# Last weighting of the first cross-attention in four pieces by queries, with spare products moved and added

## The reference

```
q = (layernorm(x) @ wq)  -> 16 heads of 64
k = (ctx @ wk)           -> 16 heads of 64
v = (ctx @ wv)           -> 16 heads of 16
attn = softmax(q k^T / 8)             # 128 queries x 12544 keys, per head
x = x + concat_heads(attn @ v)        # 128 x 256
x = x + attention(layernorm(x)) ...   # next stage, needs all of x
```

## Time and profile before

| | us |
|---|---|
| median of 3 runs | 947.75 |
| lowest, highest run | 946.58, 948.14 |
| profiled execution, its own time | 947.57 |
| its span in the trace | 945.8 |
| what lies around the span (difference) | 1.8 |
| PE busy in the span | 923.0 (98%) |
| first cross-attention in the trace | 0 to about 629 |

### The profile page before, as it was taken

One profiled execution on the slowest core, in us unless ns is written; L12 is line 12 of the kernel. 1 busy time (PEld: TensorE's weight loads), 2 busy tenths in 40 slices (PEclk: granted clock), 3 DMA queues, 4 the chain that ended last, 5 costly groups with the idle time before them and its releaser, 6 DMA issues.

```text
span 945.8 us, 30864 instructions
## 1 busy us (share of the span) xinstructions
PE 923.0 (98%) x13367; PEld 733.9 (78%) x13367; DVE 704.6 (74%) x1072; ACT 571.1 (60%) x1408; POOL 372.5 (39%) x406
## 2 busy tenths in 40 slices
PE   7999999999999999999999999989989999999998
PEld 6677777777777777777777777688978887899998
DVE  4588888888888888888888888855045554368787
ACT  5666666666666666676666666604146663346664
POOL 2644444444444444444444444301023331513332
PEclk9999999999999999999999999999989999999999
DMA  6010101111100100010100100049659897409992
GB/s 240 25 26 25 26 25 26 25 25 25 26 25 26 25 25 26 25 26 25 26 25 26 25 4 3 3 185 391 211 201 288 272 279 283 156 4 330 321 327 94
DMA packets 78555, 98.11 MB, mean 104 GB/s; under 512 B 21584, under 2 KB 56928, under 8 KB 78432
## 3 DMA queue, kind: packets, MB, share of 16 engines
q1 hardware_dynamic: 77344, 94.67, 30.8%
q10 hardware_dynamic: 1088, 1.57, 0.5%
HBM read 95.68 MB, written 0.13 MB: 101 GB/s over the span
## 4 chain that ended last, share of the span: by engine, by line
PE 95%; DVE 3%; ACT 1%; DMA 1%; issue 0%; POOL 0%; SPq 0%; DVEq 0%
PE ps L370 29%; PE ps L421 18%; PE ps L431 9%; PE ps L379 7%; PE ps L1597 6%; PE ps L1172 5%; PE ps L1074 3%; PE ps L1614 2%; PE ps L1618 2%; PE ps L1615 2%; PE ps L1161 2%; PE ps L287 1%; PE ps L1163 1%; PE ps L1162 1%; PE ps L1179 1%; DVE probsT L703 1%
## 5 line engine op out<-in xcount | busy, mean ns | idle before, releaser
L683 DVE TENSOR_REDUCE x_peak<-ps 128x1 f32<-128x512 f32 (+1 forms) x400 | 250.6, 675 | 71.3 <-PE ps L421 70.1
L598 ACT ACTIVATE probs<-ps,x_peak 128x512 f32<-128x512 f32 (+1 forms) x400 | 264.7, 712 | 35.2 <-DVE x_peak L683 35.2
L703 DVE STREAM_TRANSPOSE probsT<-probs 128x1024 f32<-128x1024 f32 (+1 forms) x200 | 225.3, 1182 | 1.8 <-ACT probs L598 1.6
L421 PE MATMUL ps<-keys,qT 64*32 64x512 f32 (+1 forms) x3200 | 219.1, 583 | 0.7 <-ACT keys L585 0.6
L585 ACT COPY keys<-ps 128x512 f32<-128x512 f32 (+1 forms) x200 | 117.7, 589 | 159.1 <-PE ps L370 159.0
L431 PEld LDWEIGHTS ps<-probsT,vals 64*32 64x32 f32 x6016 | 119.8, 106 | 86.9 <-issue 84.7
L872 POOL TENSOR_SCALAR vals<-vals_t,x_side 128x512 f32<-128x512 f32 (+1 forms) x100 | 151.9, 1536 | 51.8 <-PEq L439 51.8
L370 PE MATMUL ps<-ctxT_hi,wk_hi 128*128 128x512 f32 (+1 forms) x400 | 158.1, 395 | 0.0
L370 PE MATMUL ps<-ctxT_hi,wk_lo 128*128 128x512 f32 (+1 forms) x400 | 154.8, 387 | 0.0
L370 PE MATMUL ps<-ctxT_lo,wk_hi 128*128 128x512 f32 (+1 forms) x400 | 154.8, 387 | 0.0
L431 PE MATMUL ps<-probsT,vals 64*32 64x128 f32 x6016 | 132.9, 270 | 0.0
(11 more groups left out here) (259 smaller groups left out, 1312.7 us busy)
## 6 DMA issues: line engine op xcount, KB each, us to landing
m_w<-in_m_w SPq DMA_DIRECT2D x32, 1024.0 KB, 7.5
ctx_raw<-in_ctxT SPq DMA_DIRECT2D x24, 512.0 KB, 3.7
ctx_two<-in_ctxT SPq DMA_DIRECT2D x24, 512.0 KB, 4.3
ctx_one<-in_ctx SPq DMA_DIRECT2D x24, 512.0 KB, 5.4
x_shrinkT<-x_shrink SPq DMA_DIRECT2D x384, 1.0 KB, 1.7
f_h1T<-in_f_h1T SPq DMA_DIRECT2D x1, 4096.0 KB, 18.1
f_h2T<-in_f_h2T SPq DMA_DIRECT2D x1, 4096.0 KB, 27.8
m_shared_w<-in_m_sw SPq DMA_DIRECT2D x2, 1024.0 KB, 8.0
```

The source lines that it names most:

```text
L421: i = pe.matmul(m.ps[32 * j:32 * (j + 1), score_bank(t) + odd, 0:nt * P], m.qT[rows, 4 * group + j, qs], m.keys[rows, 4 * group + j, 0:nt ...
L598: return act.activation(m.probs[t][:, odd, 0:nt * P], m.ps[:, score_bank(t) + odd, 0:nt * P], ACT.Exp, bias=m.peak[slot][:, 1, 2 * (t // H ...
L683: dv.tensor_reduce(m.peak[slot][:, 1, 2 * (t // HALF) + odd, t % HALF:t % HALF + 1], m.ps[:, score_bank(t) + odd, 0:nt * P], AX.X, ALU.min ...
L703: i = dv.transpose(m.probsT[:, cs, 0:4 * nt, t % HALF * 32:t % HALF * 32 + 32], m.probs[t][:, :, 0:nt * P].rearrange("p c (b k) -> p c b k ...
```

## The change

`last_weighted` takes a half of the queries (`two_steps` 0 or 1) instead of all of them, so there are four calls of 64 products with 64 columns in place of two calls with 128 columns. VectorE signals `probs_turned` after steps 1, 3, 5 and 7 of the last chunk instead of after 3 and 7, and each call waits for one of these. The products with `fold` for the first half of the heads stand ahead of the last weighting, those for the second half behind it. The 19 spare products become 9, 5 and 3, in bank 0; because ScalarE reads scores from bank 0, the wait for its last exponentials moves in front of them. Six spare products are added ahead of the first layer norm's transposition.

```diff
@@ chunk, last branch
         else:
+            pe.wait_ge(s["probs_ready"], n("probs_ready", 3))
             output_turned()
-            spare_products(pe, m, OUT_BANK, 19)
+            spare_products(pe, m, 0, 9)
@@ last_weighted
-    def last_weighted(slot, first, nt):
+    def last_weighted(slot, first, two_steps, nt):
+        qs = slice(64 * two_steps, 64 * two_steps + 64)
...
-                    i = pe.matmul(m.ps[part:part + 32, OUT_BANK + two, first * 64:first * 64 + P],
-                                  m.vals[slot][rows, b, c, :], m.probsT[rows, c, b, :],
+                    i = pe.matmul(m.ps[part:part + 32, OUT_BANK + two, first * 64 + qs.start:first * 64 + qs.stop],
+                                  m.vals[slot][rows, b, c, :], m.probsT[rows, c, b, qs],
                                   start=(b < 2), stop=(b >= 4 * nt - 2), skip_group_check=True)
-        i.then_inc(s["last_full"], 1)
+        if two_steps:
+            i.then_inc(s["last_full"], 1)
+
+    def last_folded(half):
+
+        by_head = m.bank(OUT_BANK)[:, 0:D].rearrange("p (c u e) -> p c u e", c=QUADS, u=2)
+        if half:
+            pe.wait_ge(s["last_kept"], 2)
+        for u in range(2):
+            i = pe.matmul(by_head[:, 2 * half:2 * half + 2, u, :], m.last_out[:, half, u, :], m.fold[:, :],
+                          start=True, stop=True, skip_group_check=True)
+        i.then_inc(s["last_turned"], 1)
@@ last_output
+        pe.wait_ge(s["vals_ready"], n("vals_ready"))
         pe.wait_ge(s["probs_turned"], n("probs_turned"))
-        pe.wait_ge(s["vals_ready"], n("vals_ready"))
-        last_weighted(slot, 0, nt)
+        last_weighted(slot, 0, 0, nt)
+        spare_products(pe, m, 0, 5)
+        pe.wait_ge(s["probs_turned"], n("probs_turned"))
+        last_weighted(slot, 0, 1, nt)
         pe.wait_ge(s["acc_whole"], 1)
-        pe.wait_ge(s["probs_ready"], n("probs_ready", 3))
...
+        pe.wait_ge(s["last_kept"], 1)
         pe.wait_ge(s["probs_turned"], n("probs_turned"))
-        pe.wait_ge(s["last_kept"], 1)
-        last_weighted(slot, 2, nt)
+        last_weighted(slot, 2, 0, nt)
+        last_folded(0)
+        spare_products(pe, m, 0, 3)
+        pe.wait_ge(s["probs_turned"], n("probs_turned"))
+        last_weighted(slot, 2, 1, nt)
         pe.sem_inc(s["x0_read"], 1)
         pe.wait_ge(s["factors_ready"], 1)
         for j in range(4):
             by_query(j, slice(0, 2 * QUADS), m.factors, j, "factors_placed")
...
+        last_folded(1)
 
     pe.wait_ge(s["ident"], 1)
+    spare_products(pe, m, 3, 6)
     layer_norm_tensor(pe, m, s, n, 3)
@@ VectorE, chunk
-            turn_probabilities(t, CHUNK_TILES, (HALF - 1, STEPS - 1) if last else (STEPS - 1,))
+            turn_probabilities(t, CHUNK_TILES, (1, 3, 5, 7) if last else (STEPS - 1,))
@@ VectorE, outputs
-        dv.wait_ge(s["last_turned"], 1)
+        dv.wait_ge(s["last_turned"], 2)
```

## The result

The changed kernel takes 951.8 us (median of 10 runs, 950.57 to 953.96), the kernel before 947.29 us measured beside it (10 runs, 945.95 to 949.27). The ratio is 1.0045, with a 95% interval of 1.0036 to 1.0055. (Ratios here are of all runs, so they can differ a little from the ratio of two medians.) I had forecast 945.3 with a range of 943.7 to 947.8: the sign is wrong, and the time lies 4.0 us outside the range.

What follows compares the result with a forecast made beforehand. TensorE's chain was taken to bound the kernel, with 2 us of stall and half clock at the first cross-attention's end. 947.57 - 2.43 = 945.14, plus 0.18 for the median, gave 945.3 us; range 943.7 to 947.8.

Steps and rivals of the forecast that it cites:

- Rate of the pieces: Split weighting: 64-column records follow each other after 8 ns, so a piece's last record starts 1.02 us after its first.
- A: Whole change as computed: 945.3 us, own range 944.6 to 946.2 for 7 to 11 ns a record; chance 0.50.
- D: Split weighting: pieces cost by record count, 13.9 ns each, so the transposition starts 0.5 us later: 948.2 us; chance 0.12.
- rival C: Stall before the spare products: the clock falls there and half clock costs 1.46 us, giving 946.8 us; chance 0.25.
- my own sum: With half clock from 614.5: factors at 626.2, 0.6 us before 626.79; transposition gains about 1.0 us, total 946.8.
- the factors: Behind the last weighting: they start at 624.76 instead of 626.79, 2.03 us earlier.
- shape changes: TensorE's switches between products of different shape: 0.2 us charged at each one on the path.
- 1.9 us or more: Profile test on the four weighting pieces: expected about 1.3 us each; this length would show cost by record count.
- `fold` products moved ahead: Behind the last weighting: four fold records instead of eight, 0.48 instead of 0.94 us before the spare products.
- meeting of both branches: Before the transposition: VectorE and TensorE both ready at 629.44, so it starts near 629.48 instead of 631.91, 2.43 us won.
- The start: Six spare products before the first transposition: no delay, gain taken as 0, at most 1.4 us until the scores.
- 0.89 us pause: Kernel start: idle time behind the transposition remains ahead of the queries, taken as speaking against a gain from full clock.

Runs made afterwards that it cites:

- e4_half_products: Changed kernel without the start's six spare products, each piece taking only 8 of 16 blocks of keys: 945.93 us, ratio 0.9984 to the kernel before.
- e1_start_only: Kernel before plus only the six spare products ahead of the first transposition: 946.38 against 947.58 us, ratio 0.9987.
- e5_burst: Kernel before with 320 tiny products replacing the 16 spare products ahead of the second layer norm's transposition: profiled execution 972.72 us.
- e2_no_start: Changed kernel without the six spare products at the start: 954.13 us, ratio 1.0070 to the kernel before.
- e3_few_columns: Changed kernel without the start's six spare products, the four pieces' products with 8 columns instead of 64: 955.3 us, ratio 1.0082 to the kernel before.
- e10_shifted: Changed kernel plus 32 tiny products (half an instruction block) behind the first transposition: 952.51 us, ratio 1.0055 to the kernel before.
- e7_three_pieces: Changed kernel without the start's six spare products, first heads' weighting whole again, last heads' in two pieces: 949.6 against 946.61 us, ratio 1.0026.
- e11_first_stall_filled: Kernel before plus seven spare products in the 1.96 us stall behind the last scores: 946.95 us, ratio 0.9995.

## Why the prediction was wrong

**The rate of the pieces: the wrong bound.** The step "Rate of the pieces" bounded a record between 6.9 ns (columns) and 13.9 ns (count) and took 8. Measured without stops it is 10.2 ns (`e4_half_products`), up to (1.82 - 0.22) / 127 = 12.6 ns in the changed kernel's first piece. The first lies in the 7 to 11 ns of A, the second just below the 12.9 ns from which D makes the change lose. What failed is the bound itself: I let the range end at a price per record and didn't ask whether instructions arrive that fast. They arrive at 128 records in 3.5 us, 27 ns a record, twice my upper end. Rows for it lay in the trace before, in its view of the queues and in the dense stretch of 601 to 612, where transfers stand at 603.0, 607.1 and 610.5:

```profile
q8 instruction: 105, 1.72, 0.7%
```

These are 105 transfers of 16 KB. At 3.4 to 4.1 us a block the kernel before was near this edge, and four pieces of 128 records in place of two put it over.

**The clock: rival C held, beside the main cause.** In the profiled execution the clock fell behind the first stall. Nine spare products took 3.87 us against my 2.1. By my own sum that alone gives 946.8, so the rival was right on the clock and far off in the time.

**The sum, term by term.** I had the factors at 624.76; they came at 631.19, 6.4 us later, though TensorE began the first spare products 0.2 us earlier (614.34 against 614.55) and VectorE was 0.5 us earlier. On TensorE's way 6.6 us are to be explained. Stops for instructions: 2.94. Half clock in the first spare products: 1.8. Four pieces, without their stops, 1.70 to 1.82 us each instead of 1.26 to 1.29: 1.9. Together 6.6. The shape changes that I charged with 0.2 us each are in these numbers and cost no more than that.

**The rivals.** D had the right place and the right sign, but gave 948.2, since its price was that of the records alone. Its test in the profile ("1.9 us or more") would have misread the cause: the pieces take 1.7 to 1.8 us of work, and the last three take 2.6 to 2.9 us only with their stops. The chances were off mostly because I had none for a supply limit.

**Behind the stall.** The `fold` products moved ahead and the meeting of both branches were right in kind: in `e4_half_products`, which has no stops, the last piece starts at 624.66 and the factors 0.79 us later, and four `fold` records instead of eight stand ahead of the 16 spare products.

**The start.** I took 0 and kept 1.4 for the range; it is 1.2 us by the medians (`e1_start_only`), within 0.4 to 2.1. The row on the 0.89 us pause was no reason against: with a pause of 0.74 us left the key products reach full pace at about 10.3 instead of 12.5 us. But that time varies without the six products too (10.1 in `e5_burst`, 11.0 in `e4_half_products`), so how much of the 1.14 us in this pair of traces is the change's is open.

What stays open: why the stretch from one block to the next is 3.5 us (the traces only divide it, into 1.1 us to the transfer and 2.2 to 2.7 us behind it), and whether the clock's fall depends on anything in the kernel. In `e2_no_start`, `e3_few_columns` and `e10_shifted` the clock fell in, or up to 1.1 us behind, stops of 1.4 to 1.8 us, and at none of the stops of 0.86 to 1.19 us in the changed kernel and `e7_three_pieces`; but the stall of 1.71 us was followed by a fall in the kernel before and by none in `e11_first_stall_filled`, so length alone doesn't decide.

## What to carry to other kernels

Before a batch of products is split into more and narrower ones, count the instructions and hold them against the instruction transfers in the same trace: here TensorE can't use more than 256 instructions in about 3.5 us for long, or in about 6 where the DMA engines are full, whatever their columns. Stops put down to "issue" that come every 128 matmul records are that limit. What helped here was fewer instructions: half of the products (`e4_half_products`) or one block less (`e7_three_pieces`); fewer columns did not. And where two short stalls follow each other, filling one of them with spare products may only move the place where the clock falls; look at several profiles, or at the granted clock of every run, before you price it.

## What the runs showed of the hardware

I had not expected that a burst with little more than a block's instructions (150 and 166 records) already stops, and that instruction transfers slow down from 3.5 to between 5.9 and 6.8 us a block beside 400 GB/s of weights. Nor that products of 64x32 weights still take 8.2 ns a record with 8 columns, or that the clock can fall behind a stop for instructions and stay half for 10 us (`e2_no_start`, 629.1 to 639.3).
